# A graph network kernel: the stage ahead of the last edge pass unrolled with its rows in PSUM, the last node stage and the batch norm made one, and the first index tiles of each edge pass loaded during the preceding one

## What is computed

```python
h = jnp.maximum(_layernorm(x), 0.0)
x = x + _L0_gnn_ref(h, ...)      # two transformer convolutions and a skip product
h = jnp.maximum(_layernorm(x), 0.0)
x = x + _L1_gnn_ref(h, ...)      # graph attention, 4 heads, with edge features
h = jnp.maximum(_layernorm(x), 0.0)
x = x + _L2_gnn_ref(h, ...)      # two graph attentions with self loops, rows divided by their norm
h = jnp.maximum(_layernorm(x), 0.0)
x = x + _L3_gnn_ref(h, ...)      # mean, max, min and std over the edges, then a batch norm:
    mu = hc.mean(axis=0); var = hc.var(axis=0)
    out = (hc - mu) / jnp.sqrt(var + EPS_BN) * gamma + beta
```

## Time and profile before

| | us |
|---|---|
| median of 3 runs (14152.56 to 14155.51) | 14153.75 |
| the profiled execution | 14154.13 |
| its span in the profile | 14152.3 |
| GpSimd busy | 10097.0 |
| VectorE busy | 6987.7 |
| ScalarE busy | 4010.5 |
| TensorE busy | 445.7 |

### The profile page before, as it was taken

The page is one execution under the profiler, slowest core; times in us unless marked ns, Lnnn a source line. Parts: engine busy times, 40 slices in busy tenths (PEclk is TensorE's granted clock), DMA queues, the critical chain, the costliest instruction groups (busy, mean ns, idle before and its releaser), DMA issues. The chain is left out here.

```text
span 14152.3 us, 50084 instructions
## 1 busy us (share of the span) xinstructions
PE 445.7 (3%) x1759; PEld 325.1 (2%) x1759; DVE 6987.7 (49%) x10626; ACT 4010.5 (28%) x3769; POOL 10097.0 (71%) x10617
## 2 busy tenths in 40 slices
PE   1000000200000300000000000010000000000000
PEld 1000000100000200000000000000000000000000
DVE  5677776377777433333323333333333345555554
ACT  0233333233333212222112222211111114555550
POOL 4777776777777677777677777767777766777763
PEclk9999999655555655555555555555555555555555
DMA  7444444344444222222212222212222213444441
GB/s 307 108 121 116 121 116 103 90 118 118 118 119 118 49 65 63 61 63 61 54 47 60 58 60 58 60 40 58 58 60 58 60 44 130 149 151 151 157 147 46
DMA packets 1002118, 1323.16 MB, mean 93 GB/s; under 512 B 690566, under 2 KB 703750, under 8 KB 982102
## 3 DMA queue, kind: packets, MB, share of 16 engines
q0 software_dynamic: 342560, 386.08, 14.4%
q1 hardware_dynamic: 574550, 400.17, 10.2%
q10 hardware_dynamic: 84960, 536.42, 9.5%
HBM read 660.31 MB, written 661.55 MB: 93 GB/s over the span
## 5 line engine op out<-in xcount | busy, mean ns | idle before, releaser
L1713 POOL DMA_INDIRECT c_y<-g_tab,c_at x4704 | 4465.9, 949 | 1531.4 <-issue 1501.0
L707 POOL DMA_INDIRECT c_y<-h_tab,c_at x3136 | 2958.9, 944 | 1002.8 <-issue 972.2
L2083 POOL DMA_INDIRECT c_y<-h_tab,c_at x1568 | 1479.3, 943 | 580.4 <-issue 543.7
L1748 DVE TENSOR_TENSOR c_s<-c_y,c_ad 128x64 f32<-128x64 f32 x294 | 78.6, 267 | 3633.9 <-DMA c_y<-g_tab,c_at 3633.9
L1788 DVE TENSOR_TENSOR_SCAN c_acc<-c_r,c_w_in 128x1156 f32<-128x1156 f32 x294 | 754.3, 2566 | 10.2
L740 DVE TENSOR_TENSOR c_prod<-c_y,c_q_all 128x1552 f32<-128x1552 f32 x196 | 347.2, 1771 | 834.2 <-DMA c_y<-h_tab,c_at 834.2
L1808 ACT ACTIVATE c_ex<-c_de 128x64 f32<-128x64 f32 x294 | 66.9, 228 | 2419.5 <-DVE c_de L1775 2418.4
L730 DVE TENSOR_TENSOR_SCAN c_q_all<-c_mask,c_q_in 128x408 f32<-128x408 f32 (+1 forms) x784 | 733.2, 1003 | 33.0 <-issue 25.8
L771 DVE TENSOR_TENSOR_SCAN c_acc<-c_r,c_w_in 128x408 f32<-128x408 f32 (+1 forms) x784 | 732.2, 997 | 6.7
L1818 ACT ACTIVATE c_row<-c_acc 128x1088 f32<-128x1088 f32 x294 | 618.8, 2105 | 0.0
L794 ACT ACTIVATE c_q_in<-c_q_raw 128x1552 f32<-128x1552 f32 x196 | 597.5, 3049 | 67.5 <-DVE c_q_in L721 67.5
(11 more groups left out here) (369 smaller groups left out, 5566.0 us busy)
## 6 DMA issues: line engine op xcount, KB each, us to landing
rows_d<-c_row ACTq DMA_DIRECT2D x98, 2048.0 KB, 6.8
rows_d<-c_row ACTq DMA_DIRECT2D x294, 576.0 KB, 2.9
rows_d<-c_row ACTq DMA_DIRECT2D x196, 784.0 KB, 3.4
c_q_raw<-q_start SPq DMA_DIRECT2D x196, 776.0 KB, 4.5
q_start<-setup_zero SPq DMA_DIRECT2D x49, 1552.0 KB, 9.1
c_y<-h_tab,c_at POOLq DMA_INDIRECT x4704
c_y<-g_tab,c_at POOLq DMA_INDIRECT x4704, 2.5
c_y<-in_edge_attr SPq DMA_DIRECT2D x196, 256.0 KB
```

The lines of the kernel that those rows point to most:

```text
L707: nc.gpsimd.indirect_dma_start(y[:, b, k, 0:D], None, h_tab, indexed(at[:, b, k:k + 1]))\
L1713: nc.gpsimd.indirect_dma_start(y[:, b, k, :], None, g_tab, indexed(at[:, b, k:k + 1]))\
L2083: nc.gpsimd.indirect_dma_start(y[:, b, k, :], None, h_tab, indexed(at[:, b, k:k + 1]))\
```

## The change

1. Index tiles. `at` is one tile kept through the kernel. `setup` loads blocks 0 and 1 of it, and each pass but the last loads them again at its end for the next one, when the last use has passed. GpSimd's wait is then for `i * 16` instead of `i * 16 + 16`. The edge attributes of the first two blocks are loaded ahead of the loop. `start_d` and `last_d` are gone, and `prepare_conv`'s loop over index tiles is unrolled and reads `start_i`. `gat_to_gat` and `conv_to_gat` no longer wait for their scatters at the end. `gat_edges` has SP do so ahead of `ad_raw`.

```diff
+    at = keep("at", [P, 2, G], I32)
...
+                for b in range(2):
+                    sp.dma_start(at[:, b], sources(b)).then_inc(at_loaded[b].h, 16)
...
+                for g in range(NBLK):
+                    b = g % 2
+                    pool.wait_ge(*q_ready[b](g // 2 + 1))
+                    pool.nop(nofuse=True)
+                    for k in range(NB):
+                        c = g * NB + k
+                        nc.gpsimd.indirect_dma_start(q_start, indexed(start_i[:, c:c + 1]), qs[:, b, k, :],
+                                                     None).then_inc(scattered[b].h, 16)
...
+                for b in range(2):
+                    sp.wait_ge(*weighted[b](half))
+                    sp.dma_start(at[:, b], sources(b)).then_inc(at_loaded[b].h, 16)
...
             sp.wait_ge(*tab(16 * NBLOCK))
-            sp.wait_ge(*scattered(16 * NC))
...
+                def edge_attrs(i, b):
...
+
+                sp.wait_ge(*signals["scattered0"](0))
                 sp.dma_start(ad_raw[:], by_edge(ad_start)).then_inc(ad_loaded.h, 16)
-                with sp.Fori(0, half) as i:
+                for b in range(2):
+                    edge_attrs(0, b)
+                with sp.Fori(1, half) as i:
                     for b in range(2):
-                        g = i * 2 + b
                         sp.wait_ge(*weighted[b](i))
-                        sp.dma_start(at[:, b], a["src"].rearrange("(p t) -> p t", p=P)[:, bass.ds(g * G, G)])\
-                            .then_inc(at_loaded[b].h, 16)
+                        sp.dma_start(at[:, b], sources(i * 2 + b)).then_inc(at_loaded[b].h, 16)
                         if bd is not None:
                             sp.wait_ge(*e_scored[b](i))
-                            sp.dma_start(ea[:, b, :], a["edge_attr_8"][bass.ds(g * P, P), :])\
-                                .then_inc(e_loaded[b].h, 16)
+                        edge_attrs(i, b)
+                for b in range(2):
+                    sp.wait_ge(*weighted[b](half))
+                    sp.dma_start(at[:, b], sources(b)).then_inc(at_loaded[b].h, 16)
...
-                        pool.wait_ge(*at_loaded[b](i * 16 + 16))
+                        pool.wait_ge(*at_loaded[b](i * 16))
```

```diff
+    def gat_to_pna(tag, rows, bias, gt):
...
+        J1, NBUF = JG + 1, 3
+        blocks = [(c, min(14, NC - c)) for c in range(0, NC - 14, 14)] + [(NC - 14, 8), (NC - 6, 6)]
...
+        got = st.sb("got", [P, NBUF, 14, TG])
...
+            lsum scale centre square var lroot rinv done""".split()
...
+                    sp.wait_ge(*steps((i + 1) * len(names)))
+                    sp.dma_start(by_node(h_tab)[:, c:c + n, :], h[:, c:c + n, :]).then_inc(tab.h, 16)
+                sp.wait_ge(*tab(16 * len(blocks)))
...
+
+                        pool.wait_ge(*before(i - NBUF, "own"))
+                        pool.nop(nofuse=True)
+                    for k in range(n):
+                        nc.gpsimd.indirect_dma_start(got[:, i % NBUF, k, :], None, rows,
+                                                     indexed(last_i[:, c + k:c + k + 1]))\
+                            .then_inc(node_got[i % NBUF].h, 16)
...
+                for i, (c, n) in enumerate(blocks):
+                    act.wait_ge(*before(i, "exp"))
+                    act.activation(exps(n), de[:, :, 0:n, :], ACT.Exp).then_inc(steps.h, 1)
+                    act.wait_ge(*before(i, "sq"))
+                    act.activation(own[:, 0:n, :], ps_o[:, 0:n, :], ACT.Square).then_inc(steps.h, 1)
+                    act.wait_ge(*before(i, "root"))
+                    act.activation(nrm[:, 0:n], nrm[:, 0:n], ACT.Sqrt).then_inc(steps.h, 1)
+                    act.wait_ge(*before(i, "square"))
+                    act.activation(own[:, 0:n, :], ps_o[:, 0:n, :], ACT.Square).then_inc(steps.h, 1)
+                    act.wait_ge(*before(i, "lroot"))
+                    act.activation(sd[:, 0:n], var[:, 0:n], ACT.Sqrt, bias=eps[:], scale=1.0 / D).then_inc(steps.h, 1)
...
+                                              de[:, :, 0:n, :])
...
+                    v.wait_ge(*before(i, "w1"))
+                    v.tensor_tensor(ex[:, 0], ex[:, 0], r, ALU.mult).then_inc(steps.h, 1)
+                    v.wait_ge(*before(i, "w2"))
+                    v.tensor_tensor(ex[:, 1], ex[:, 1], r, ALU.mult).then_inc(steps.h, 1)
+                    v.wait_ge(*before(i, "accw"))
+                    v.tensor_tensor(split(o), acc, wide(ex[:, 0]), ALU.mult).then_inc(steps.h, 1)
+                    v.wait_ge(*before(i, "own"))
+                    v.tensor_tensor(split(own_), split(gt[:, cols, 0:D]), wide(ex[:, 1]), ALU.mult).then_inc(steps.h, 1)
+                    v.wait_ge(*before(i, "sum"))
+                    v.tensor_tensor(o, o, own_, ALU.add).then_inc(steps.h, 1)
+                    v.wait_ge(*before(i, "bias"))
+                    v.tensor_tensor(o, o, bv[:].unsqueeze(1).to_broadcast([P, n, D]), ALU.add).then_inc(steps.h, 1)
+                    v.wait_ge(*before(i, "ssum"))
+                    v.reduce_sum(nrm[:, 0:n], own_, axis=AX.X).then_inc(steps.h, 1)
...
+                    v.wait_ge(*before(i, "addx"))
+                    v.tensor_tensor(x[:, cols, :], x[:, cols, :], o, ALU.add).then_inc(steps.h, 1)
+                    v.wait_ge(*before(i, "lsum"))
+                    v.reduce_sum(mu[:, 0:n], x[:, cols, :], axis=AX.X).then_inc(steps.h, 1)
+                    v.wait_ge(*before(i, "scale"))
+                    v.tensor_scalar(mean, mu[:, 0:n], 1.0 / D, None, ALU.mult).then_inc(steps.h, 1)
+                    v.wait_ge(*before(i, "centre"))
+                    v.tensor_tensor(o, x[:, cols, :], row(mean), ALU.subtract).then_inc(steps.h, 1)
+                    v.wait_ge(*before(i, "var"))
+                    v.reduce_sum(var[:, 0:n], own_, axis=AX.X).then_inc(steps.h, 1)
+                    v.wait_ge(*before(i, "rinv"))
+                    v.reciprocal(rs[:, 0:n], sd[:, 0:n]).then_inc(steps.h, 1)
```

```diff
+        got = st.sb("got", [P, NBUF, NW, 4 * D])
...
+        mean, msq = (st.ps(n, [P, 1024])[:, 0:W].rearrange("p (k f) -> p k f", k=NW) for n in ("mean", "msq"))
+        small, sum_ps, sq_ps = (st.ps(n, [P, 512]) for n in ("small", "sum_ps", "sq_ps"))
+        rdeg, beta = small[:, 0:NC], small[:, NC:NC + D]
...
+                for g, cols in enumerate(blocks):
+                    sp.wait_ge(*written(g + 1))
+                    sp.dma_start(by_part[0:cut, cols, :], x[0:cut, cols, :]).then_inc(stored.h, 16)
+                    sp.dma_start(by_part[cut:full, cols, :], x[cut:full, cols, :]).then_inc(stored.h, 16)
+                    if cols.start < rest:
+                        own = slice(cols.start, min(cols.stop, rest))
+                        sp.dma_start(tail[:, own, :], x[full:full + 1, own, :]).then_inc(stored.h, 16)
...
+                    if g >= NBUF:
+
+                        pool.wait_ge(*after(g - NBUF, "min"))
...
+                    act.wait_ge(*before(g, "sq"))
+                    act.activation(t[:], mean, ACT.Square).then_inc(steps.h, 1)
...
+                for g, cols in enumerate(blocks):
+                    act.wait_ge(*centred(g + 1))
+                    act.activation(sq[:, cols, :], h[:, cols, :], ACT.Square).then_inc(squared.h, 1)
...
+                def add_columns(total, values, cols):
+                    for part, rows_ in pieces(cols):
+                        n = (part.stop - part.start) * D
+                        last = nc.tensor.matmul(total[:, 0:n], ones[0:rows_, :],
+                                                values[0:rows_, part, :].rearrange("p c f -> p (c f)"),
+                                                start=part.start == 0, stop=part.stop == NC)
+                    return last
+
+                for g, cols in enumerate(blocks):
+                    pe.wait_ge(*after(g, "h13"))
+                    pe.nop(nofuse=True)
+                    add_columns(sum_ps, h, cols).then_inc(summed.h, 1)
+                for g, cols in enumerate(blocks):
+                    pe.wait_ge(*squared(g + 1))
+                    pe.nop(nofuse=True)
+                    add_columns(sq_ps, sq, cols).then_inc(sq_summed.h, 1)
...
+                    v.wait_ge(*before(g, "xb"))
+                    v.tensor_tensor(x[:, cols, :], x[:, cols, :], beta.unsqueeze(1).to_broadcast([P, NW, D]),
+                                    ALU.add).then_inc(steps.h, 1)
...
+                v.wait_ge(*steps(len(names) * NWBLK))
+                for cols in blocks:
+                    v.tensor_tensor(h[:, cols, :], h[:, cols, :], wide(mu[:]), ALU.subtract).then_inc(centred.h, 1)
...
+                for g, cols in enumerate(blocks):
+                    v.tensor_tensor(h[:, cols, :], h[:, cols, :], wide(sc[:]), ALU.mult).then_inc(scaled.h, 1)
+                    if g:
+                        v.wait_ge(*scaled(g))
+                        v.tensor_tensor(x[:, blocks[g - 1], :], x[:, blocks[g - 1], :], h[:, blocks[g - 1], :],
```

(1 more changed line is left out.)

513 lines of the change are left out of this document (178 added, 335 removed).

## The result

The changed kernel took 13929.65 us (13928.14 to 13932.98, 4 runs) against 14153.15 us; the ratio is 0.9842 with a 95% interval of 0.983 to 0.9854. The forecast was 13933, in a range of 13912 to 13970.

The account below looks back on a forecast made before the run. GpSimd, mostly its gathers, was taken to bound the kernel, with gains between passes and at the end: 147.7 + 16.4 + 29.5 + 26.5 + 0.6 = 220.7, so 14153.75 - 220.7 = 13933 us, range 13912 to 13970.

Parts of the forecast that it names:

- The end: Last `h` of the sixth node stage to the kernel's end: 43.3 us instead of 191.05, minus 147.7.
- The column sums of the last block: After the last `h`, on TensorE: 896 columns at the low clock level, 3.3 us.
- rival (d): Output store: its pieces still go through one DMA engine each, end 103 us longer, 14036 us; chance 0.03.
- The sixth node stage: Gathers start 2.4 us earlier and lose their stalls, 13.9 us: minus 16.4.
- The fifth node stage: Earlier start 3.4, shorter VectorE blocks 17.0, quicker way into pass 6 9.1: minus 29.5 us.
- The attention passes: Three passes whose first gathers no longer wait for index tiles behind `ad_raw`: minus 26.5 us.
- Rival (a): Attention passes: gathers issued beside `ad_raw` stall GpSimd, the 26.5 us are not gained, 13960 us; chance 0.2.
- The wait for the scatters: Stage ends, wait moved to SP ahead of `ad_raw`: GpSimd is waited for anyway, so nothing gained.
- (c): Batch norm at the end: TensorE stays at the low clock level for the squares, plus 8, 13941 us; chance 0.1.
- (e): Edge blocks: index tiles load later and GpSimd pays; from 0.43 us a block slower than before, 14186 us; chance 0.02.
- the convolution passes: Two passes with the same index-tile wait, 0.35 us each: minus 0.6 us.

Follow-up runs that it names:

- e7_after: The changed kernel itself, unedited, rerun on another chip for comparison: 13925.63 us against 14155.16 for the kernel before, ratio 0.9838.
- e1_out112: Kernel before, with the output stored as 112 partitions, then 15, then the last one: 14039.49 us against 14146.89, ratio 0.9924.
- e2_out113: Kernel before, with the output stored as 113 partitions, then 14, then the last one: 14161.65 us in one run.
- e2_outcols: Kernel before, with the 127-partition output cut by nodes into seven transfers: 15500.07 us in one run against 15504.02.
- e11_sbuf: Changed kernel with the PSUM tiles of both node stages back in SBUF, on a second chip: 15307.52 us against 15499.52 for the kernel before, ratio 0.9878.
- e5_sbuf: Changed kernel with the PSUM tiles of both node stages back in SBUF: 15312.3 us against 15504.02 for the kernel before, ratio 0.9873.
- e6_beta: Changed kernel with beta read from SBUF in the sixth node stage and two buffers instead of three in the fifth: 15282.3 us in one run.
- e4_scatter_wait: Changed kernel with the wait for the scatters put back at the end of the node stages: 13921.54 us, ratio 0.9841.

## Why the prediction was right, step by step

**The end** was forecast at 43.3 us and took 41.2. The column sums of the last block took 3.32 as said, and from there to TensorE's first square 3.2. The squares took 13.6 (15 was taken): a granted clock of 0.52 for 5.9 us, 1.00 for the rest, and the windows of the kernel before had shown both levels. The sum's prices were too high here. It priced each block by products that stand alone (1.91 and 1.02 us for 512 columns). Each such product is two instructions in the trace, and back to back one starts 0.43 us after the other at the high level and 0.85 at the low one. So seven blocks of 896 columns would take some 10.5 and 20.9 us, an estimate from these starts, and not 12.5 and 23.4. `e7_after` took 12.20 with a part at the low level, below the forecast's bound. That the 15 lay so near is partly luck. Scale and add took 14.1, not 15.8: I had added the gap of 0.03 us that stands between two dependent operations to each, but here the next one waits for nothing and starts every 1.00 us, before the last has ended. The tail from the last add took 4.6 and not 3.7. SP needs 0.3 to 0.5 us for each DMA, and the last block has two. The errors of 1.4, 1.7 and -0.9 make up the 2.1, but for rounding. `e1_out112` shows the largest term by itself: 107 of the 149.8 us that the end gave back are this one edit of the output, and rival (d) is out by it, `e2_out113` and `e2_outcols`. The rule of the Trainium skill that the prediction cites for it agrees with all four counts.

**The sixth node stage.** First gather 2.3 us earlier (2.4 forecast). The gathers' stretch is 13.15 us shorter (13.9). `e11_sbuf` and `e5_sbuf`, with `e6_beta` beside them, show that PSUM is what does it. The gathers average 953 ns and not the 945 of the fifth stage, because six of them are still held by L2335, by 0.64 us in all. The rule of the Trainium skill ("SBUF — State Buffer", "Who interferes with whom") has the right sides. Its sentence that whoever issues first holds the port agrees with the gathers that are held only where VectorE began first, but the traces do not agree that the other is then blocked: an operation of VectorE that begins with a gather or during one is at most 0.04 us longer. They fit a gather that needs the port at its begin alone, and not for its 0.94 us; it decides between 0.2 and 0.9 us for an operation. The prediction looked at `tensor_tensor` alone and had no price for L2335.

**The fifth node stage.** 3.3 us earlier (3.4), 142.2 us from the first block's arrival to the last `h` (142.5), then 3.3 to pass 6 (3.4). VectorE bounds it as said, with 19.3 us a block; GpSimd is done with the last gather 39 us before.

**The attention passes.** -27.2 against -26.5, which is nearer than the reasoning deserves. The 0.9 us that I took off in each for the way into the loop are not there: the first gather into `y` comes 0.30 us behind (7233.60). On the page the idle time of these gathers, issue apart, fell from 30.4 us to 0.3, while their busy time and issue rose by 3.1 (4468.0 and 1502.0 against 4465.9 and 1501.0), which no term has. That is within what chips and executions differ by: the same three passes took 6018.7 us here and 6012.7 in `e4_scatter_wait`. Undoing the part on one chip costs 29.3 in the passes, and on the chip of `e2_outcols` and `e6_beta` they differ by 30.1. So the gain is the sum without the deduction, and two small errors cancelled in the 27.2. Rival (a) falls: in the fourth edge pass the eight gathers into `y` issued while `ad_raw` loads take 0.94 to 0.96 us. The four in each attention pass that the scans hold take 2.95 to 3.20, and took 3.05 to 3.25 before.

**The wait for the scatters** was right at nothing. **(c)** was half true, 5.9 us at the low level, at a price that lies inside the 15. **(e)** did not happen: the gathers of the passes are as long as before (950 ns and 949).

**The total** was met to 3 us (13933 and 13929.65). That it is so close is luck in part. In the traces the end gave 2.1 us more than said and the attention passes 0.7 more, while the sixth stage's gathers gave 0.75 less, the fifth stage with the way into pass 6 0.4 less and the convolution passes 0.3 less. The mechanism was right in every stage, and the small errors partly cancelled.

## What to carry to other kernels

Look at the number of partitions of each transfer: 127 goes through one DMA engine and 112 through sixteen, and splitting off 15 partitions was worth 107 us here, half of all. Where GpSimd bounds a stage, keep one input of VectorE's wide `tensor_tensor` operations in PSUM; where VectorE bounds it, choose the blocks by its cost per block and per node, small ones first. Load what a stage needs first in the stage ahead, if its load would stand behind a large one in a queue.
